# Output weights centred by VectorE, fewer bias matmuls, causal masks in 32-row tiles, and a new order of steps in a four-layer attention kernel

## The reference

```python
# L0: x [16,64,128], ctx [16,64,128]
x = LN(x + attn(x, x) @ sa_out_w.T + sa_out_b) * ln1_g + ln1_b            # "sa"
x = LN(x + attn(x, ctx; keys with (s - head) % 4 == 0) @ ca_o_w.T + ca_o_b)...   # "ca"
x = LN(x + gelu(x @ w1.T + b1) @ w2.T + b2)...                            # "f"
# L1: keys = values = ctx @ W_token + b_token, keys masked by mask_BxS2
x = LN(x + concat([x, attn @ W_out + b_out]) @ W_upd + b_upd)...          # "l1"
# L2: causal
a = LN(x + causal_attn(x, ctx));  x = a + gelu(a @ W1.T + b1) @ W2.T + b2 # "l2", "g"
# L3: scores' relu squared inside a band given by the token indices
x = x + (w / max(sum w, eps)) @ v @ Wo.T                                   # "l3"
```

## Time and profile before

| | |
|---|---|
| median of 3 runs | 187.59 us (186.73 to 188.26) |
| the profiled execution, its own time | 188.99 us |
| its span, first to last instruction | 187.1 us |
| granted TensorE clock, mean | 1.000 |
| busy: PE / DVE / ACT / POOL | 175.3 / 134.9 / 117.7 / 38.1 us |
| DMA | 6.24 MB, nearly all in the first 17 us |

### The profile page before, as it was taken

The page is one execution under the profiler, slowest core; times in us unless marked ns, Lnnn a source line. Parts: engine busy times, 40 slices in busy tenths (PEclk is TensorE's granted clock), DMA queues, the critical chain, the costliest instruction groups (busy, mean ns, idle before and its releaser), DMA issues.

```text
span 187.1 us, 10262 instructions
## 1 busy us (share of the span) xinstructions
PE 175.3 (94%) x4535; PEld 132.1 (71%) x4535; DVE 134.9 (72%) x278; ACT 117.7 (63%) x293; POOL 38.1 (20%) x55
## 2 busy tenths in 40 slices
PE   7889979999899999999999987999979999999995
PEld 3458658777778889778866765677547776777783
DVE  4799947887656898396168988268889459867881
ACT  3357425677777975776883645659386847565663
POOL 8920070414201106301101034103230101100000
PEclk9999999999999999999999999999999999999999
DMA  5997000000000000000000000000000000000012
GB/s 127 307 403 251 4 4 4 5 5 7 4 4 4 4 0 0 5 4 0 5 7 4 4 5 4 4 4 4 4 5 4 4 4 7 0 4 5 25 38 60
DMA packets 4347, 6.24 MB, mean 33 GB/s; under 512 B 592, under 2 KB 3664, under 8 KB 4048
## 3 DMA queue, kind: packets, MB, share of 16 engines
q1 hardware_dynamic: 3872, 5.43, 8.7%
q10 hardware_dynamic: 432, 0.17, 0.3%
HBM read 5.07 MB, written 0.52 MB: 30 GB/s over the span
## 4 chain that ended last, share of the span: by engine, by line
PE 82%; DVE 6%; issue 5%; ACT 3%; DMA 2%; ACTq 0%; POOL 0%; POOLq 0%; DVEq 0%
PE bank L359 39%; PE score L362 22%; PE bank L362 12%; PE bank L584 6%; DVE m_col_sb L945 3%; DMA small_sb<-in_small 2%; PE bank L492 1%; DVE k_heads_sb L872 1%; ACT L803 1%; PE bank L645 1%; ACT probs_sb L724 1%; PE bank L689 1%; DVE att_sb L1020 0%; PE bank L440 0%; ACT hid_sb L803 0%
## 5 line engine op out<-in xcount | busy, mean ns | idle before, releaser
L1117 POOL TENSOR_TENSOR rstd_sb<-var_sb,half_sb 128x2 f32<-128x2 f32 x20 | 15.1, 755 | 106.2 <-ACT att_sb L786 79.2
L724 ACT ACTIVATE probs_sb<-score 128x1024 f32<-128x1024 f32 (+1 forms) x28 | 25.9, 961 | 15.8 <-PE score L362 15.6
L945 DVE TENSOR_REDUCE m_col_sb<-score 128x32 f32<-128x2048 f32 (+1 forms) x16 | 30.2, 1890 | 5.8 <-PE score L362 5.2
L359 PEld LDWEIGHTS bank<-v_ext_sb,probs_sb 128*32 128x32 f32 x2112 | 22.2, 110 | 9.5 <-issue 7.9
L359 PE MATMUL bank<-v_ext_sb,probs_sb 128*32 128x18 f32 (+1 forms) x2112 | 26.1, 189 | 1.3 <-issue 1.3
L362 PE MATMUL score<-q_heads_sb,k_kept_sb 32*64 32x256 f32 x512 | 20.1, 386 | 1.0 <-issue 1.0
L359 PE MATMUL bank<-xa_sb,W_sb 128*128 128x256 f32 x62 | 18.4, 409 | 0.4 <-ACT k_kept_sb L749 0.2
L1025 DVE TENSOR_TENSOR att_sb<-bank,rstd_sb 128x256 f32<-128x256 f32 x16 | 6.8, 423 | 14.4 <-POOL rstd_sb L1117 14.3
L786 ACT ACTIVATE att_sb<-bank,eps_sb 128x128 f32<-128x128 f32 x32 | 11.5, 366 | 9.0 <-PE bank L362 8.9
L886 DVE TENSOR_TENSOR q_heads_sb<-q_kept_sb,small_sb 128x1024 f32<-128x1024 f32 x12 | 14.8, 1237 | 0.7 <-ACT q_kept_sb L738 0.7
L584 PE MATMUL bank<-W_sb,att_sb 128*128 128x128 f32 x71 | 14.1, 286 | 1.3 <-DVE att_sb L1020 1.2
(11 more groups left out here) (164 smaller groups left out, 346.0 us busy)
## 6 DMA issues: line engine op xcount, KB each, us to landing
W_sb<-in_mats SPq DMA_DIRECT2D x1, 1088.0 KB, 8.0
W_sb<-in_mats SPq DMA_DIRECT2D x1, 1024.0 KB, 10.1
ctxT_sb<-in_ctxT SPq DMA_DIRECT2D x1, 512.0 KB, 5.5
cn_sb<-in_ctx SPq DMA_DIRECT2D x1, 512.0 KB, 11.3
hid_sb<-in_idx SPq DMA_DIRECT2D x1, 512.0 KB, 6.8
out<-attT_sb SPq DMA_DIRECT2D x3, 128.0 KB, 1.8
xa_sb<-in_xT SPq DMA_DIRECT2D x2, 128.0 KB, 3.2
xa_sb<-in_xT SPq DMA_DIRECT2D x1, 256.0 KB, 4.3
```

What stands on the lines that cost most here:

```text
L359: return pe.matmul(o, l, r, start=start, stop=stop)
L724: act.activation(dst, src, ACT.Exp, scale=SCALE).then_inc(sem("exp"), 1)
L945: dve.tensor_reduce(o, src, AX.X, ALU.max).then_inc(sem("max"), 1)
L1117: pool.tensor_tensor(rstd[:, g, :], var[:, g, :], half[:, 0:NJ], ALU.pow).then_inc(sem("rstd"), 1)
```

## The change

1. `weights` 0 and 1 are gone from TensorE. The host stores the matrices transposed (`sa_o`, `ca_o`, `l1_upd`, `l1_upds`, `f_w2_*`), so that the mean to be taken out runs along the free axis, and VectorE does it: a sum, a scaling, a subtraction over four matrices at once, and for i = 0 an addition of the identity first. The `WC` that comes out is the same.
2. `weights` 3 is 4 matmuls (one of 4 columns, three of one) in place of 7, and VectorE adds the two parts.
3. The masks of `l2` are 16 matmuls of 32 rows and 256 columns in place of 8 of 64 rows and 512; rows whose pattern would need a 33rd row use one row as a constant. In `s` both halves of one tile follow each other; in `t` all tiles' first halves come before the second. The pattern array grows from 192 to 320 columns.
4. `warm` lies in `probs`; `COLS` is reordered.
5. `SCHEDULE` is another list of nearly the same steps (two lines of it below).

```diff
@@ SCHEDULE
-k/sa q/sa q_kept/sa k_heads/sa q_heads/sa k/sa/1 k_kept/sa/1 k_heads/sa/1 k_kept/sa identb v_base/sa s/sa max/sa
+v_base/sa identb k/sa k_heads/sa q/sa q_kept/sa q_heads/sa sel k/sa/1 k_kept/sa/1 v_base/ca s/sa q/sa/2 q/sa/1
...
@@ weights(i), TensorE
-                if i == 0:
-                    pe.wait_ge(sem("w1_loaded"), 16)
-                    pe.wait_ge(sem("w2_loaded"), 16)
-                    for c, n in enumerate(["sa_o", "ca_o", "l1_updT"]):
-                        mm(o[:, c * 128:(c + 1) * 128], mat(n), mat("center"))
-                    mm(o[:, 384:512], mat("l1_updsT"), mat("center"), stop=False)
-                    last = mm(o[:, 384:512], mat("ident"), mat("center"), start=False)
-                elif i == 1:
...
-                    for c in range(F_CHUNKS):
-                        last = mm(o[:, c * 128:(c + 1) * 128], mat(f"f_w2_{c}"), mat("center"))
...
-                        for n, (b, m) in enumerate(terms):
-                            last = mm(o[:, c:c + 1], m, col(b), start=n == 0, stop=n == len(terms) - 1)
+                    at = COLS.index("sa_ob")
+                    mm(o[:, 0:len(SHIFT)], mat("center"), V[:, at:at + len(SHIFT)])
+                    for c, (b, n) in enumerate((("sa_vb", "sa"), ("ca_vb", "ca"), ("l1_ob", "l1_upd"))):
+                        last = mm(o[:, 4 + c:5 + c], WC[:, WC_OF[n], :], col(b))
@@ scores, TensorE
-                                part = rows_of(r // 2, 64)
-                                mm_onto(o.rearrange("p j h k -> p (j h) k"), pattern("same")[part, :],
-                                        pattern("later")[part, :].unsqueeze(1).to_broadcast([64, NJ * HH, T]), start=True)
+                                for c in range(2):
+                                    mm_onto(o.rearrange("p j h k -> p (j h) k")[:, :, 32 * c:32 * c + 32],
+                                            pattern(f"query_{c}")[rows_of(r), :], pattern("later")[rows_of(r), :]
+                                            .unsqueeze(1).to_broadcast([32, NJ * HH, 32]), start=c == 0)
@@ scores_t, TensorE
-                    for x, r in tiles:
-                        part = rows_of(r // 2, 64)
...
+                    for c in range(2):
+                        for x, r in tiles:
+                            mm_onto(place(x, r).rearrange("p j h q -> p (j h) q")[:, :, 32 * c:32 * c + 32],
+                                    pattern(f"key_{c}")[rows_of(r), :], pattern("earlier")[rows_of(r), :]
+                                    .unsqueeze(1).to_broadcast([32, NJ * HH, 32]), start=c == 0)
@@ weights_kept(i), VectorE
+                if i < 2:
+                    dve.wait_ge(sem("w2_loaded" if i == 0 else "w3_loaded"), 16)
...
+                        dve.tensor_tensor(mat("l1_upds"), mat("l1_upds"), mat("ident"), ALU.add).then_inc(sem("residual"), 1)
...
+                    dve.tensor_reduce(weight_total[:, four], w, AX.X, ALU.add).then_inc(sem("weight_total"), 1)
...
+                    dve.tensor_scalar(weight_mean[:, four], weight_total[:, four], 1.0 / D, None, ALU.mult
+                                      ).then_inc(sem("weight_mean"), 1)
...
+                    last = dve.tensor_tensor(WC[:, four, :], w, weight_mean[:, four].unsqueeze(2)
+                                             .to_broadcast([128, 4, 128]), ALU.subtract)
...
-                if i < 2:
-                    last = dve.tensor_copy(WC[:, 4 * i:4 * i + 4, :].rearrange("p a n -> p (a n)"), o[:, :])
...
-                    dve.tensor_copy(shift[:], o[:, 0:len(SHIFT)])
+                    dve.tensor_copy(shift[:], o[:, 0:len(SHIFT)]).then_inc(sem("shift"), 1)
+                    dve.wait_ge(sem("shift"), 1)
+                    dve.tensor_tensor(shift[:, 0:3], shift[:, 0:3], o[:, 4:7], ALU.add).then_inc(sem("shift"), 1)
```

More of the change, by code:

```diff
@@ L114 @@
[L114 to L118, removed]
@@ new lines @@
+z/sa m_row/sa/2 av/sa/1/1 divide/sa/1 var/sa rstd/sa scale/sa t/sa/2 exp/sa/2 k/ca/2 k_heads/ca/2 flip/sa/1
+attT/sa/1 flip_x/sa exp/sa/2/1 m/sa/3 av/sa/2 m_row/sa/3 shifted/sa/1 z/sa/1 var/sa/1 rstd/sa/1 ln/sa q_heads/sa/3
+t/sa/3 av/sa/2/1 q/ca exp/sa/3 q_kept/ca band k/ca/3 exp/sa/3/1 scale/sa/1 flip_x/sa/1 ln/sa/1 divide/sa/2 flip/sa/2
+attT/sa/2 k_heads/ca/3 v/ca gammas v_even/ca av/sa/3 s/ca max/ca max_parts/ca q/ca/1 q_kept/ca/1 z/sa/2 var/sa/2
+s/ca/1 max/ca/1 m/ca m_row/ca av/sa/3/1 v/l1 max_parts/ca/1 v_odd/l1 m/ca/1 m_row/ca/1 t/ca exp/ca divide/sa/3
@@ new lines @@
+h/f/2/1 ln/f/1 q/l1/1 ln/ca/3 h/f/3 q_kept/l1/1 max_parts/l1 gelu/f/2/1 s/l1/1 m/l1 z/f/2 gelu/f/3 q_heads/l1
+m_row/l1 var/f/2 h/f/3/1 rstd/f/2 max/l1/1 max_parts/l1/1 m/l1/1 t/l1 gelu/f/3/1 m_row/l1/1 q_heads/l1/1 scale/f/2
+flip_x/f/2 exp/l1 z/f/3 ctx_scale k/l2/1 ln/f/2 exp/l1/0/1 var/f/3 rstd/f/3 av/l1 k_kept/l2/1 q/l1/2 q_kept/l1/2
+t/l1/1 exp/l1/1 exp/l1/1/1 av/l1/0/1 k/l2/2 k_kept/l2/2 scale/f/3 flip_x/f/3 ctx_rows//1 ctx_normed//1 divide/l1
+q_heads/l1/2 flip/l1 attT/l1 ln/f/3 s/l1/2 max/l1/2 z/l1 av/l1/1 q/l1/3 var/l1 ctx_rows//2 q_kept/l1/3 av/l1/1/1
@@ new lines @@
+ctx_normed//2 max_parts/l1/2 s/l1/3 rstd/l1 scale/l1 m/l1/2 flip_x/l1 m_row/l1/2 ln/l1 k/l2/3 k_kept/l2/3 k/l3/2
+k_kept/l3/2 divide/l1/1 flip/l1/1 attT/l1/1 max/l1/3 k_heads/l2/2 q/l2 q_kept/l2 max_parts/l1/3 ctx_rows//3
+ctx_normed//3 k_heads/l2/3 t/l1/2 exp/l1/2 q_heads/l2 z/l1/1 ctx_rows av/l1/2 exp/l1/2/1 m/l1/3 q_heads/l1/3
+var/l1/1 rstd/l1/1 ctx_normed x4_rows/l2 av/l1/2/1 divide/l1/2 s/l2 flip/l1/2 v/l3 scale/l1/1 x4_rows/l2/1
+flip_x/l1/1 attT/l1/2 z/l1/2 v_odd/l3 ln/l1/1 m_row/l1/3 max/l2 max_parts/l2 var/l1/2 q/l2/1 q_kept/l2/1 t/l1/3
@@ new lines @@
+exp/l1/3 v_even/l3 k/l3 rstd/l1/2 scale/l1/2 x4_rows/l2/2 flip_x/l1/2 k/l3/1 exp/l1/3/1 av/l1/3 k_heads/l2/1 s/l2/1
+k_kept/l3 ln/l1/2 q/l2/2 k_kept/l3/1 m/l2 max/l2/1 q_kept/l2/2 v/l3/1 v_odd/l3/1 v_even/l3/1 m_row/l2 av/l1/3/1
+divide/l1/3 max_parts/l2/1 v/l3/2 v_odd/l3/2 v_even/l3/2 t/l2 flip/l1/3 v/l2 q_heads/l2/1 v/l2/1 attT/l1/3
+v_even/l2/1 z/l1/3 exp/l2 exp/l2/0/1 v_even/l2 var/l1/3 q_heads/l2/2 rstd/l1/3 scale/l1/3 s/l2/2 max/l2/2 v_odd/l2
+av/l2 v_odd/l2/1 av/l2/0/1 divide/l2 stats/l2 max_parts/l2/2 flip_x/l1/3 ln/l1/3 m/l2/1 m_row/l2/1 q/l2/3
@@ L298, in pattern @@
         def pattern(n):
[L299 removed]
+            a0, w = PATTERNS[n]
+            return patb[:, a0:a0 + w]
         def X(x):
```

151 lines of the change are left out of this document (75 added, 76 removed).

## The result

The changed kernel takes 202.05 us (median of 4, 198.35 to 203.48), the kernel before 187.93 beside it: a ratio of 1.065, 95% interval 1.045 to 1.086. The forecast was 183.3, so sign and size were wrong. The kernel before was timed again beside every group of experiments; the groups ran on different chips, and its medians are 187.6 to 189.9. In some executions of every kernel, that before too, the granted clock is lower and the time some per cent longer, and the ratios given here leave these out.

What follows compares the result with a forecast made beforehand. TensorE was taken to bound the kernel (busy 175.3 of 187.1 us), VectorE from 6 to 20 us. Terms -2.4 + 0.5 - 0.4 - 2.0 = -4.3 from 188.99 gave 184.7, times 0.9926 183.3 us; 8-in-10 range 179.8 to 187.0.

Steps and rivals of the forecast that it cites:

- Masks, -2.4: Eight mask steps of l2, all on the chain, each to fall from 0.56 to 0.26 us: 2.4 us saved.
- the rival of blocked pairs: In `s`, two masks of one tile block each other, 1.1 us a step in place of 0.56: 186.7 us; chance 0.06.
- the 0.28 of half the columns: Mask step of l2: half the columns in twice as many tiles leave half of 0.56 us, saving 2.2 us in all.
- the near twin: Key masks of l1's transposed scores, also 16 bf16 matmuls of 256 columns, 0.24 us: the model for the new mask step.
- The first stretch, +0.5: First centring, self-attention: VectorE's added work delays TensorE, bias gain included; +0.5 us, bounds -0.7 and +1.3.
- The second centring, -0.4: TensorE loses four matmuls, -1.0 us; VectorE's centring before cross-attention's maxima of group 3 is partly exposed, +0.6; together -0.4.
- the +0.6: Cross-attention, group 3: of VectorE's 1.5 us centring 0.9 is covered, 0.6 us is not; bounds 0 and 1.5.
- The order, -2.0: The rest of the new list: fewer queues and waits of TensorE for others, -2.0 us, the least certain term.
- The slower rival: Both centring stretches: VectorE's centring wholly exposed, 5.1 us against 4.1 saved, the order losing 1.5: 190.1 us; chance 0.06.

Runs made afterwards that it cites:

- fill_late: The changed kernel plus three dead fp32 matmuls, two behind the scores of group 2 and one before the first transposed scores: 197.60 us against 202.05.
- old_order_tiny: The changed code with the list of before, the removed matmuls put back as tiny dead ones: 193.30 us, 1.035 of the kernel before.
- before_new_order: The kernel before with the new list, its two centrings on TensorE put straight ahead of VectorE's copies: 199.63 us against 188.61, 1.056.
- the fills: Three versions of the changed kernel with five, two or three dead matmuls added where TensorE waited early: 196.83, 197.04 and 197.60 us against 202.05.
- after_pad128: The changed kernel with 128 tiny dead instructions and one warm matmul less at its start: 201.52 us, 1.064 of the kernel before.
- before_masks: The kernel before with the masks of l2 in 32 rows, and `warm` in `probs`: 193.11 us, 1.022 of the kernel before.

## Why the prediction was wrong

**The accounting.** Take fill_late for the changed kernel without half clock: 194.0 - 187.1 = +6.9, of which busy -4.0 (with 1.7 of dead fill in it, so -5.7 by the change), border waits +7.4, other waits +3.5. The changed kernel's own 201.0 is 7.0 above that, and 27.3 us at half clock by 0.30 are 8.2. By the ratios (times 187.6 us) the change was to save 4.3 us and cost 12.2. Of these 16.5 us, 6.6 are missed with the old list already (1.023 measured, 0.988 by the sum without its order term), and 9.9 come with the new one.

**The step that failed: TensorE's own issue waits and its clock were taken as fixed.** The prediction says that the granted clock is 1.000 throughout, "so nothing is to be had there", and that the 5% of issue time is a thing "which no order removes". It is true that nothing was to be had, but much was to be lost. The issue time was in good part border waits, 3.1 us in the kernel before; the masks alone move them to 6.5, the new list alone to 6.2, 62 instructions alone to 7.6, the whole change to 8.7. And the changed kernel is at half clock for 27 us in its profile and 10 to 24 in its other executions. Neither had a term in the sum.

**Masks, -2.4: right in the steps, wrong in the time.** Eight steps at 0.22 to 0.25, so 8 x 0.32 = 2.6, in `s` as in `t`; the rival of blocked pairs is refuted. But the masks alone made the kernel 4.2 us slower (1.022). From -2.4 that is 6.6 us, the whole of what is missed with the old list: the 128 instructions that they add were counted as nothing. Between the 0.28 of half the columns and the near twin's 0.24, the twin was right.

**The first stretch, +0.5: right in VectorE's row, wrong in what its idleness does.** VectorE's timeline in the changed kernel:

```profile
12.46 2.28 DVE L958 TENSOR_REDUCE m_col_sb<-score 128x32 f32<-128x2048 f32 x1
14.66 0.28 DVE L822 TENSOR_TENSOR W_sb<-W_sb 128x128 f32<-128x128 f32 x1
14.98 0.69 DVE L827 TENSOR_REDUCE weight_total_sb<-W_sb 128x4 f32<-128x512 f32 x1
15.70 0.17 DVE L829 TENSOR_SCALAR weight_mean_sb<-weight_total_sb 128x4 f32<-128x4 f32 x1
15.90 0.69 DVE L832 TENSOR_TENSOR WC_sb<-W_sb,weight_mean_sb 128x512 f32<-128x512 f32 x1
16.84 2.28 DVE L958 TENSOR_REDUCE m_col_sb<-score 128x32 f32<-128x2048 f32 x1
```

0.28 + 0.69 + 0.17 + 0.69 = 1.83 us, forecast 1.8; the first transposed scores start at 20.03, forecast 20.7. One wait of TensorE for it was missed: 0.77 us at 15.92. I counted TensorE's 1.21 us there as worth nothing. With them gone and the new list, TensorE waits in three places before 18 us, and then runs at half clock for 20 us; neither alone does this in its profile (old_order_tiny, before_new_order), and whether the missing matmuls are to blame no run shows.

**The second centring, -0.4.** In the changed kernel it runs from 65.42 to 67.03, between the maxima of group 2 and those of group 3 of cross-attention as drawn. VectorE then still waits 0.53 us for the scores of group 3, and TensorE shows no wait there; the +0.6 did not arise. Both centrings together, at equal borders and in the old list, came to +0.2 by the medians (193.30 - 193.11) and +2.4 by the ratios (1.035 - 1.022), forecast +0.1: the size stays open.

**The order, -2.0 with bounds of +1.5 and -5: outside its bounds.** In the changed code the new list costs +6.2 by the medians (202.05 - 195.81) and +7.9 by the ratios. Its waits for other engines are indeed 1.8 us less, nearly the term; what overruns it are the border waits and the half clock above. In the code of before, though, the same list has 5.1 us more of other waits, so the -1.8 does not belong to the list alone.

**The slower rival** (190.1, VectorE wholly exposed) had the right sign, but the runs bear it out in small part only: 0.77 us of wait at the first place, none at the second, at most 3.0 us at equal borders. Its own sum is wrong too: 1.3 + 1.5 + 0.3 + 1.24 + 2 x 0.85 is 6.0 and not 5.1, which makes it 191.0, still 11 us below what was measured.

**What stays open.** What exactly takes the clock. before_new_order has one wait of 2.08 us from 14.8 and keeps 1.00; the changed kernel has 2.2 us in three pieces and falls; the fills have 2.1 to 2.6 us of waits there and avoid the long fall; fill_late has a border wait of 2.15 us at 47.5 and keeps 1.00, where the changed kernel falls for 3 us behind one of 2.13; and executions of one and the same kernel differ (27 and 10 us at half clock for the changed one, 31 and 4 for after_pad128). Also open is a rule that tells a good pad from a bad one beforehand.

## What to carry to other kernels

When a trace shows waits on "issue" in the middle of a burst, number the engine's instructions: if the waits end at one place of each 256, the time depends on where the borders lie, and any edit that adds or removes instructions must be judged at several alignments, or beside a version with dead instructions that restores the count. Read the granted clock of several executions before and after, not of one: here a change that removed TensorE work left it busy for longer, because part of it ran at the lower level. And measure a new list apart from new code; here each was slow alone.

## What was unexpected of the hardware

- TensorE's instructions come in blocks of 16 KB (256), one load of about 1 us each, and work resumed 2.4 to 2.8 us after such a load had begun in the waits listed. In the four costliest waits of the changed kernel the load began 2.7 to 3.2 us (in most others 0.6 to 1.4) after the block before had been entered; why it began late there, no run tells.
- 62 more instructions, which themselves take half a microsecond, made a kernel of 188 us slower by 6%; 144 and 112 dead instructions at the start of before_masks were 7.7 us apart (190.15 and 197.81).
- Dead matmuls made a kernel faster by 2 to 5 us, and its profiles kept the upper clock where it had fallen, though TensorE's waits were not filled. A microsecond at the lower level goes with 0.3 us of time between executions of the changed kernel and 0.48 between those of the kernel before.
